# Indirect transfers in another order on one queue, two index groups in place of three, and idle-time products on TensorE

## What is computed

```python
probs = jax.nn.softmax(xf @ gate_w.T + gate_b, axis=-1)
topw, topi = jax.lax.top_k(probs, TOPK)             # TOPK = 2 of NE = 8
...
sel_w, sel_idx = jax.lax.top_k(wm.T, cap)           # cap = int(1.2 * 2048 / 8) = 307 tokens per expert
xg = xf[sel_idx]
h = gelu(einsum('ecd,edh->ech', xg, w1) + b1)       # 128 -> 512
out = einsum('ech,ehd->ecd', h, w2) + b2            # 512 -> 128
of = zeros((T, D)).at[sel_idx].add(out * sel_w)     # each token sums the experts that chose it
```

## Time and profile before

| what | us |
|---|---|
| median of 3 runs | 160.93 (160.16 to 161.36) |
| the profiled execution's own time | 160.53 |
| its span, from first to last instruction | 158.8 |
| outside the span | 1.73 |

### The profile page before, as it was taken

The page is one execution under the profiler, slowest core; times in us unless marked ns, Lnnn a source line. Parts: engine busy times, 40 slices in busy tenths (PEclk is TensorE's granted clock), DMA queues, the critical chain, the costliest instruction groups (busy, mean ns, idle before and its releaser), DMA issues.

```text
span 158.8 us, 2492 instructions
## 1 busy us (share of the span) xinstructions
PE 122.4 (77%) x855; PEld 92.8 (58%) x855; DVE 85.4 (54%) x332; ACT 52.0 (33%) x141; POOL 70.8 (45%) x124
## 2 busy tenths in 40 slices
PE   6699999998795876779775899799491999994000
PEld 2377999997661443344673687687460868874000
DVE  2567789776779888878751104163201435334361
ACT  4299777661179700000000324045001340450000
POOL 7985365457340000002077767567772524356100
PEclk9999999999999789999965599999969789999755
DMA  3579999500000000082002221202120000115597
GB/s 116 141 187 401 301 301 399 208 0 4 0 0 2 4 0 0 0 265 55 0 19 56 60 56 47 58 33 58 54 56 33 20 32 17 33 45 165 169 278 222
DMA packets 15596, 15.46 MB, mean 97 GB/s; under 512 B 1816, under 2 KB 12224, under 8 KB 15584
## 3 DMA queue, kind: packets, MB, share of 16 engines
q1 hardware_dynamic: 14240, 12.45, 25.1%
q0 software_dynamic: 1344, 2.86, 6.3%
HBM read 9.67 MB, written 5.64 MB: 96 GB/s over the span
## 4 chain that ended last, share of the span: by engine, by line
PE 43%; issue 22%; ACT 9%; another core or an unknown queue 8%; DMA 7%; POOL 3%; DVE 3%; SPq 3%; POOLq 0%; DVEq 0%
PE bank L1131 14%; PE bank L1115 10%; PE bank L946 4%; ACT rows L569 4%; DMA xb<-parts 3%; PE bank L973 2%; PE bank L986 2%; DMA vecs<-in_L_conv_k_beta_dram 2%; PE bank L976 2%; PE bank L941 2%; DMA parts<-y_tail,tail_rows 1%; PE bank L959 1%; ACT hid L588 1%; PE bank L1109 1%
## 5 line engine op out<-in xcount | busy, mean ns | idle before, releaser
L1131 PE MATMUL bank<-w_sb,hid 128*128 128x128 f32 (+1 forms) x192 | 27.7, 298 | 6.3 <-ACT hid L588 3.4
L1131 PEld LDWEIGHTS bank<-w_sb,hid 128*128 128x128 f32 (+1 forms) x192 | 23.7, 178 | 8.7 <-DVE y_tail L880 3.5
L588 ACT ACTIVATE hid<-bank,b1T 128x307 f32<-128x307 f32 x32 | 15.6, 518 | 38.9 <-PE bank L1115 26.5
L481 POOL DMA_INDIRECT parts<-q_work,kv x16 | 15.7, 980 | 16.7 <-DVE q_work L880 13.3
L923 PE MATMUL bank<-warm_rhs 128*128 128x512 bf16 x76 | 21.3, 412 | 1.4 <-POOL warm_rhs L359 1.4
L1115 PE MATMUL bank<-xgT,w_sb 128*128 128x307 f32 x64 | 21.2, 480 | 0.6 <-ACT xgT L574 0.6
L463 POOL DMA_INDIRECT kv<-table,index x16 | 16.5, 1033 | 10.0 <-DVE index L850 5.4
L880 DVE SCALAR_TENSOR_TENSOR q_work<-bank,kv,wb 128x128 f32<-128x128 f32 x16 | 5.6, 351 | 23.7 <-PE bank L1131 21.3
L1115 PEld LDWEIGHTS bank<-xgT,w_sb 128*128 128x128 f32 x64 | 13.1, 217 | 6.6 <-issue 3.8
L1050 PEld LDWEIGHTS bank<-hits,ones 128*128 128x128 bf16 x160 | 6.1, 102 | 12.7 <-DVE hits L779 10.1
L494 POOL DMA_INDIRECT w_h<-table,first_rows x1 | 1.2, 1189 | 27.4 <-DMA table<-rows 27.4
(11 more groups left out here) (197 smaller groups left out, 238.2 us busy)
## 6 DMA issues: line engine op xcount, KB each, us to landing
w_sb<-in_L_ffn_w_dram SPq DMA_DIRECT2D x1, 2048.0 KB, 10.5
parts<-zeros SPq DMA_DIRECT2D x4, 512.0 KB, 7.7
table<-rows SPq DMA_DIRECT2D x1, 1152.0 KB, 5.9
x_sb<-parts SPq DMA_DIRECT2D x4, 256.0 KB, 3.1
xb<-parts SPq DMA_DIRECT2D x4, 256.0 KB, 4.5
out_dram<-att SPq DMA_DIRECT2D x4, 256.0 KB, 2.5
x_sb<-in_x_dram SPq DMA_DIRECT2D x1, 512.0 KB, 4.6
b_sb<-in_L_ffn_b_dram SPq DMA_DIRECT2D x1, 512.0 KB, 18.3
```

Of the source, the lines that this page charges most:

```text
L481: pool.indirect_dma_start(out=parts, out_offset=bass.IndirectOffsetOnAxis(ap=xg_rows[:, e // 2, at, C + E + e:C + E + e + 1], axis=0), in_ ...
L588: act.activation(hid[:, e % 2, c, :], ps_h[c][:, 0:CAP], ACT.Gelu, bias=b1T[:, e * HC + c:e * HC + c + 1]).then_inc(h_ready, 1)
L1131: ins = pe.matmul(ps_ys[(NC * e + k) % 2][y_at:y_at + n, 0:C], hid[:, e % 2, c, at:at + n], w2_sb[:, e, c, :], start=(c == 0), stop=(c == ...
```

## The change

Three edits. POOL issues all 20 gathers first and then all 21 puts. The experts form two index groups of four, so the first group's patterns are twice as large, the number of `find`, `grid`, `spread` and `index` steps falls from three of each to two, and the PSUM banks of the third group fall away; `copy_index(0)` now stands ahead of `onehot_maj(1)` on DVE. And PE gets 13 idle-time products between the steps of the index lists and around `tokens_in(0)`.

```diff
-    GROUPS = ((0, 2), (2, 4), (4, 8))
+    GROUPS = ((0, 4), (4, 8))
...
-    GATHERS_AFTER = (10, 3, 4, 3)
...
-        ps_grids = [banks[6], banks[4], banks[7]]
-        ps_indexes = [banks[3], banks[5], banks[6]]
-        ps_tails = [banks[0], banks[0], banks[4]]
+        ps_grids = [banks[6], banks[7]]
+        ps_indexes = [banks[3], banks[6]]
+        ps_tails = [banks[0], banks[4]]
...
-            assert sum(GATHERS_AFTER) == len(order)
-            done = 0
-            for e in range(-1, E):
-                if e >= 0:
-                    put(e)
-                n = GATHERS_AFTER[e + 1] if e + 1 < len(GATHERS_AFTER) else 0
-                for next_e, c in order[done:done + n]:
-                    gather(next_e, c)
-                done += n
+            for e, c in order:
+                gather(e, c)
+            for e in range(E):
+                put(e)
...
             onehot_tok(1)
             copy_grid(0)
+            copy_index(0)
             onehot_maj(1)
-            copy_index(0)
-            onehot_tok(2)
             copy_grid(1)
-            onehot_maj(2)
             copy_index(1)
-            copy_grid(2)
-            copy_index(2)
...
+            keep_warm(ps_kv, 1)
             spread_tokens(0)
+            keep_warm(ps_kv, 4)
             find_tokens(1)
+            keep_warm(ps_kv, 1)
             spread_tokens(1)
-            find_tokens(2)
-            spread_tokens(2)
+            keep_warm(ps_kv, 7)
             tokens_in(0)
+            keep_warm(ps_kv, 1)
```

## The result

The changed kernel takes 168.11 us in the median of four runs (167.65 to 168.61); the kernel before took 160.93 beside it (160.16 to 161.36, three runs). Executions that ran at a lower clock and some per cent longer, here one of the kernel before (164.31 us), are left out of the medians and ratios of this document. The ratio is 1.045, interval 1.039 to 1.052: 4.5% slower. Forecast were 152.9 us, in a range up to 166. It is rival (c), a little stronger than priced.

The account below looks back on a forecast made before the run. The expert loop was taken to set the end, losing 10.6 us to late PE signals. +0.15 - 1.75 - 10.6 + 4.2 = -8.0 gave 152.5 us, or 152.9 on the median's scale; range 147.7 to 166.

Parts of the forecast that it names:

- rival (c): Expert loop: POOL's missing pauses keep PE's signals late through experts 1 to 4; slower, 166.7 us; chance 0.20.
- POOL's order, indirectly: -6.4 us: Expert loop: late PE signals cost 1.4 us for each of experts 1 to 3, 4.2 in place of 10.6.
- the long standstill: Loss of 9.2 us between `down(3)` and `down(5)` in the kernel before, where puts and gathers alternate without a pause.
- two standstills: Loss of 18.4 us in the expert loop, the upper end for POOL's indirect effect, giving 166.7 us.
- the first unbroken row: POOL's first ten gathers without a pause in the kernel before, said to have cost expert 0 nothing.
- POOL's order directly nothing: POOL's queue: gathers end at 105.7 us, and the later puts hold up nobody, with 2.3 us of cover.
- the products: 13 idle-time products on PE ahead of the expert loop: they hold the clock at full, -1.7 us.
- The lists: Index lists ahead of the gathers: twice the patterns in the first group delay the first gather by about 0.6 us.
- The hold by DVE's compare: First gathers: DVE's 2048-wide compare holds the first by 0.6 us, in place of 1.0 on the second; +0.15 in all.
- the port rule: VectorE and GpSimd share an exclusive port pair; GpSimd can't write descriptors during a two-port VectorE operation; 0.6 us counted.
- (b): Expert loop: one long standstill stays and only moves; 157.5 to 160.3 us, 2% faster or no change; chance 0.25.
- The end: From the last put's start to the end of the execution's time: 14.3 us, untouched by the change.

Follow-up runs that it names:

- the experiments with waits and memsets: Changed kernel with POOL stopping its transfers: one wait for expert 0's results, 164.34 us; waits for landing behind gathers 10 and 15, 166.25; memsets there instead, 165.79.
- the old POOL order: Changed kernel with gathers between puts again (10, 3, 4, 3), keeping two index groups and the 13 idle-time products: 163.64 us in two runs.
- two memset pauses: Changed kernel with two 128 x 1024 memsets on POOL behind its 10th and again behind its 15th gather: 165.79 us, ratio 1.022.

## Why the prediction was wrong

**The step that failed is "POOL's order, indirectly: -6.4 us".** It priced the lateness at 1.4 us for each of experts 1 to 3, 4.2 us in all, because it read the long standstill as belonging to the alternation of puts and gathers. The runs show that the alternation is not needed: gathers alone make it (the kernel before with all gathers first, 17.5 us), and so does a row of spare gathers elsewhere. What counts is how long POOL goes on issuing at a pitch of 1.36 us or less; at 1.55 little is lost. The change made the longest such row, 79.78 to 106.16 us. Measured: 18.9 us lost in place of 4.2, +14.7.

**Rival (c) named it.** Its pauses "that let PE's signals through" are what the experiments with waits and memsets show, and its point, a loss of over 12.2 us, was passed. Its price of two standstills, 18.4, is 0.5 off. What was held against it, that the first unbroken row cost expert 0 nothing, was a matter of time: in the kernel before POOL's tenth gather ended at 93.22 us, and expert 0's first two chunks, ready near 93 and 94, were taken up at 93.34 and 95.44. The second was late already, by 1.5 us, and only cost nothing. With `down(0)` 1.5 us earlier expert 0 waits as well, even in the old POOL order (2.74 us). The range stopped just short of (c)'s 166.7; 0.5 us more of loss, 1.2 at the end, less 0.4 in front give the 168.0.

**Right.** `up(0)` took 2.31 us, forecast 2.3. POOL's order directly nothing: the 20th gather ended at 104.85, forecast 105.7, and no time was lost because POOL came late to a put.

**Right in number, wrong in mechanism.** `down(0)` started at 89.93, forecast 90.3. But the products did not hold the clock, which read 0.6 and 0.5 from 79.0 to 87.3 us where the prediction wanted 9; they only brought it back ahead of `up(0)`. The transposes, forecast 0.3 us shorter, still took 0.91 at half the clock, and the seven products in front of them 3.17 us. The third gather made up for it: it started at 82.69 in place of the forecast 83.7. That the two met within 0.4 us is in part luck.

**Mis-sized.** The lists: the first gather starts at 79.78, forecast 80.35. One profile can't judge that, since the start lies between 79.8 and 82.5 us in executions of versions with the very same lists. The hold by DVE's compare: the compare runs at 79.09 to 80.31 and the first gather, begun at 79.78, takes 1.35 us in place of 0.94, so 0.4 where 0.6 stood. The prediction added its 0.6 to a first gather of 1.18 us, which was itself 0.24 longer than most, beside DVE's `oh_tok` from 79.53 to 80.09; so it forecast 1.78 us where 1.35 were measured. These rows agree with the port rule that the prediction cites from the Trainium skill in "SBUF — State Buffer", section "SBUF: two separate sides": here and in the kernel before, the held gather ends 0.8 us behind the end of DVE's compare (81.13 behind 80.31, 83.21 behind 82.40). The other rule that it cites from the Trainium skill, in "TensorE: Matmul & The Clock Gate", section "The cost: per-tile semaphore tail", some 26 ns for a product's signal, would have had all signals in time. From expert 3 on they are: DVE takes up its third chunk within 0.1 us of PE's last product. In POOL's rows they are late by up to 16 us. The chances are added up a little wrong: with somewhat under half of (b)'s 0.25 counted as faster, more than the stated 0.14 is left within 1%, and slower gets at most 0.20.

**The end.** Forecast at 14.3 us from the last put, measured 15.5: the last loads from `parts` take 5.26 us in place of 4.80, and SP starts them later behind the put. No experiment was made on it.

**Still open.** What falls behind while indirect transfers follow each other at 1.25 us, and why PE's signals are late and DVE's are not. The runs fit a unit that serves both and falls behind, but none shows it. Nor is it shown what sets the onset: in the changed kernel the signals up to 90.0 us come in time, though the gathers run from 79.78 on, and no run varied PE's work alone. The pitch was raised only by memsets, so a longer pitch without work on POOL is untested. Every time here comes from executions that were also recorded by the profiler; one without was not made, so whether the recording has a part in the lateness is open too.

## What to carry to other kernels

A chain piece of several us without a releaser, PE's finished chunks taken up later and later, the last ones a few us behind the break, and an engine that issues indirect transfers without a break beside it belong together: look for the break, not for the work. Such transfers have to be counted and paced, since each one cost nearly the same here at 32 or 128 rows and at 64 or 576 bytes a row; 0.3 us of other work behind most of them was worth some 13 us (168.1 to 155.5), while two pauses of 2 us only moved the standstill. And a coincidence in time that a prediction notices deserves the price of its worst case, when the change makes just that stretch longer.

## What the runs showed of the hardware

- Indirect transfers on POOL's queue take 0.94 us each and 0.30 to the next (128 rows), 0.86 and 0.30 (32 rows); plain ones some 0.55 us each (3.28 for six).
- In a row at a pitch of 1.17 to 1.36 us, beside PE's products, PE's signals to ACT and DVE came up to 16 us late (16.0 in the kernel before with gathers first); at 1.55 us they came within 2.4 us, and mostly at once. Some came through inside a row. Behind a row of ten gathers the first came out 1.2 to 2.0 us after its end, with POOL idle or busy with memsets; behind the long rows the last came 2 to 4 us after.
- The same bytes by plain transfers made none late, with six on SP's queue over 10.3 us or six on POOL's queue in 3.28 us.
- With the same instructions on PE ahead of the loop, the granted clock fell to 0.50 from 80.2 to 87.0 us in one execution and stayed at 1.00 in another (two memset pauses); the same seven products took 3.17 and 1.68 us.
